# Layer-0 experts and combination: gather rings of eight places instead of four, and another row for the empty places

## The reference

```python
# layer 0, FFN: 32 experts, each token goes to one
logits = xf @ router_w.T + router_b
idx = jnp.argmax(logits, axis=-1)
h = jax.nn.relu(jnp.einsum('nd,ndh->nh', xf, W1[idx]) + b1[idx])      # 256 -> 64
out = jax.nn.relu(jnp.einsum('nh,nhd->nd', h, W2[idx]) + b2[idx])     # 64 -> 256
x = x + out
# layer 1, graph part: three convolutions with the same normalised adjacency A
h1 = layernorm(x) @ W1 + b1 ; n1 = layernorm(relu(A @ h1) + h1) ...
```

## Time and profile before

| | |
|---|---|
| time, median of 3 runs | 2222.27 us (2222.09 to 2224.4) |
| span of the profiled execution | 2275.9 us |
| PE busy | 1915.3 us, 84% of the span |
| DVE busy | 1555.9 us, 68% |
| ACT busy | 1080.4 us, 47% |
| POOL busy | 433.7 us, 19% |

### The profile page before, as it was taken

How to read it: one execution, slowest core, us unless ns; L and a number is a source line. 1 busy time by engine, 2 the same in 40 slices (tenths; PEclk the granted TensorE clock), 3 DMA queues, 4 the chain that set the end, 5 groups by cost and what they waited for, 6 DMA issues and landing times.

```text
span 2275.9 us, 41877 instructions
## 1 busy us (share of the span) xinstructions
PE 1915.3 (84%) x15580; PEld 1273.2 (56%) x15580; DVE 1555.9 (68%) x3262; ACT 1080.4 (47%) x2170; POOL 433.7 (19%) x517
## 2 busy tenths in 40 slices
PE   6999386899999998938994989578867999999787
PEld 3777253678887887826662777456653222222333
DVE  7866654667777667764567557543576999998554
ACT  7555265633443344426674555255554233232654
POOL 0000564100000012216642110055510000000000
PEclk9999688999999999969996999789988999999898
DMA  7999457568888879864567364522232333232000
GB/s 204 309 342 337 114 138 145 201 232 324 310 321 314 308 273 374 332 227 153 191 202 255 105 170 143 181 85 79 73 121 61 119 117 90 82 91 77 1 25 25
DMA packets 238299, 412.55 MB, mean 181 GB/s; under 512 B 20496, under 2 KB 189072, under 8 KB 219857
## 3 DMA queue, kind: packets, MB, share of 16 engines
q1 hardware_dynamic: 214836, 361.52, 47.4%
q0 software_dynamic: 13760, 39.68, 6.5%
q10 hardware_dynamic: 9504, 8.65, 1.2%
HBM read 316.02 MB, written 93.78 MB: 180 GB/s over the span
## 4 chain that ended last, share of the span: by engine, by line
PE 48%; DVE 26%; DMA 9%; ACT 8%; issue 6%; SPq 1%; POOL 1%; ACTq 0%; another core or an unknown queue 0%; DVEq 0%; POOLq 0%
DVE BIG L3024 7%; PE ps L1098 6%; PE ps L1100 6%; PE ps L1099 6%; PE ps L292 5%; PE ps L294 4%; PE ps L293 4%; PE ps L2846 4%; PE ps L2494 4%; DMA BIG<-in_adjT 3%; PE ps L2852 2%; DMA BIG<-in_adj 2%; PE ps L2496 2%; DMA X<-rows_split,idxg 1%; DVE BIG L1644 1%
## 5 line engine op out<-in xcount | busy, mean ns | idle before, releaser
L1098 PE MATMUL ps<-R,BIG 128*128 128x256 f16 (+1 forms) x1764 | 484.1, 274 | 3.0 <-ACT BIG L1539 2.4
L1100 PE MATMUL ps<-R,BIG 128*128 128x256 f16 (+1 forms) x1764 | 481.5, 273 | 0.0
L1099 PE MATMUL ps<-R,BIG 128*128 128x256 f16 x1764 | 481.1, 273 | 0.0
L2846 PE MATMUL ps<-BIG 128*64 128x452 f32 x1056 | 231.2, 559 | 23.9 <-DVE BIG L3024 20.1
L3024 DVE SCALAR_TENSOR_TENSOR BIG<-BIG 128x904 f32<-128x904 f32 x176 | 192.4, 1155 | 1.6
L1098 PEld LDWEIGHTS ps<-R,BIG 128*128 128x128 f16 x1764 | 171.1, 97 | 29.9 <-issue 2.7
L1099 PEld LDWEIGHTS ps<-R,BIG 128*128 128x128 f16 x1764 | 173.1, 98 | 21.2 <-issue 0.3
L1100 PEld LDWEIGHTS ps<-R,BIG 128*128 128x128 f16 x1764 | 171.3, 97 | 23.9
L2908 ACT ACTIVATE BIG<-X,BIG 128x64 f32<-128x64 f32 x264 | 70.2, 337 | 233.8 <-PE ps L2852 233.8
L2557 DVE TENSOR_TENSOR X<-R,X 128x512 f16<-128x512 f32 (+1 forms) x116 | 72.8, 627 | 142.8 <-ACT X L2535 117.0
L2846 PEld LDWEIGHTS ps<-BIG 128*64 128x64 f32 x1056 | 64.5, 137 | 187.4 <-issue 132.0
(11 more groups left out here) (447 smaller groups left out, 4407.3 us busy)
## 6 DMA issues: line engine op xcount, KB each, us to landing
BIG<-adj_split SPq DMA_DIRECT2D x63, 1376.0 KB
BIG<-in_adjT SPq DMA_DIRECT2D x42, 1408.0 KB, 11.8
BIG<-in_adj SPq DMA_DIRECT2D x22, 1408.0 KB
BIG<-in_adjT SPq DMA_DIRECT2D x66, 452.0 KB, 3.3
adj_split<-BIG SPq DMA_DIRECT2D x21, 1376.0 KB
XX<-in_f SPq DMA_DIRECT2D x70, 256.0 KB, 8.8
experts_split<-XX SPq DMA_DIRECT2D x64, 256.0 KB
BIG<-experts_split SPq DMA_DIRECT2D x16, 1024.0 KB
```

The source lines that it names most:

```text
L1098: pe.matmul(out[:, 0:n], pr[:, 0, k, :], h[:, k, 0:n], start=start, stop=False)
L1099: pe.matmul(out[:, 0:D], pr[:, 0, k, :], l[:, k, 0:D], start=False, stop=False)
L1100: return pe.matmul(out[:, 0:n], pr[:, 1, k, :], h[:, k, 0:n], start=False, stop=stop)
L2846: pe.matmul(ps[rs, 2 * (h // 2) + c, 0:CW], self.G[:, u, h * HF:(h + 1) * HF], self.PT[:, u, h, cs], start=start, stop=stop)
```

## The change

- `xg` and `yg1` have eight places each, with a semaphore for each (g0 to g7). Gather j of the experts waits for the transposes of tile j-8, gather t of C0 for the pair (t-8)//2. `xg` takes 1024 more columns of X2, and the work areas behind it move up by as much.
- In the expert stage POOL issues eight gathers, not four, before Degrees and `W[1].pool`.
- An empty place reads the row of its own partition (place p reads row p), in all three routes. That is one more DVE instruction, and one more wait on DVE's own semaphore, ahead of `idxg`.
- Degrees and Many (a small stage of layer 1) use semaphores that other stages also use, in place of six of their own.

```diff
+GATHERED = tuple(f"g{u}" for u in range(8))
-        yg1 = BIG[:, YG:YG + 1024].rearrange("p (u n) -> p u n", u=4)
+        yg1 = BIG[:, YG:YG + 2048].rearrange("p (u n) -> p u n", u=8)
-        xg = work(0, 1024, F16).rearrange("p (u n) -> p u n", u=4)
+        xg = work(0, 2048, F16).rearrange("p (u n) -> p u n", u=8)
...
# C0.pool
-                    if t >= 4:
-                        s.wait(pool, "ta", (t - 4) // 2 + 1)
-                    pool.indirect_dma_start(yg1[:, t % 4, :], None, ys_dram[0:TILES[E0] * P, :],
+                    if t >= 8:
+                        s.wait(pool, "ta", (t - 8) // 2 + 1)
+                    pool.indirect_dma_start(yg1[:, t % 8, :], None, ys_dram[0:TILES[E0] * P, :],
...
# Route.dve; a is -1 at an empty place, pos1 is the partition's number plus 1
                 if A == 1:
-                    v.tensor_scalar(idxg[:, 0:J], a, 0.0, None, ALU.max).then_inc(s["ix"], 1)
+                    link(v.tensor_scalar(c, a, 0.0, pos1[:, 0:1], ALU.is_lt, ALU.mult))
+                    v.tensor_tensor(idxg[:, 0:J], a, c, ALU.add).then_inc(s["ix"], 1)
...
-                v.tensor_scalar(idxg[:, 0:J], b, 0.0, None, ALU.max).then_inc(s["ix"], 1)
+                link(v.tensor_scalar(c, a, 0.0, pos1[:, 0:1], ALU.is_lt, ALU.mult))
+                v.tensor_tensor(idxg[:, 0:J], b, c, ALU.add).then_inc(s["ix"], 1)
...
# Degrees (Many in the same way)
-                self.st = Stage("deg", d=1, r=1, ok=1)
-                self.done = [self.st.end("ok")]
+                self.st = Stage("seq", qp=1, qs=1, pz=1)
+                self.done = [self.st.end("pz")]
...
# Experts0.pool
                 def gather(j):
-                    if j >= 4:
-                        s.wait(pool, "t3", j - 3)
-                    pool.indirect_dma_start(xg[:, j % 4, :], None, xrows[:, :],
+                    s.wait(pool, "t3", j - 7)
+                    pool.indirect_dma_start(xg[:, j % 8, :], None, xrows[:, :],
...
-                for j in range(4):
+                for j in range(8):
                     gather(j)
                 deg.pool(pool)
                 W[1].pool(pool)
-                for j in range(4, self.J):
+                for j in range(8, self.J):
                     gather(j)
```

More of the change, by code:

```diff
@@ L220, in work @@
             return v if dt == F32 else v.bitcast(dt)
-        xg = work(0, 1024, F16).rearrange("p (u n) -> p u n", u=4)
[L223 to L227, removed]
+        xg = work(0, 2048, F16).rearrange("p (u n) -> p u n", u=8)
+        xf = work(2048, 512, F16).rearrange("p (u i n) -> p u i n", u=2, i=4)
+        hact = work(2560, 1024).rearrange("p (u t n) -> p u t n", u=2, t=4)
+        hh = work(3584, 512, F16).rearrange("p (u t n) -> p u t n", u=2, t=4)
+        hl = work(4096, 512, F16).rearrange("p (u t n) -> p u t n", u=2, t=4)
+        yo = work(4608, 1024).rearrange("p (u n) -> p u n", u=4)
         tval = work(0, 2 * KT * JMAX, F16)
@@ L696, in __init__ @@
             def __init__(self, experts, route):
-                n = 16 * (KT // 4)
-                self.st = Stage("seq", g0=n + 16, g1=n + 16, g2=n, g3=n, ta=PR, ag=PR, le=PR, rs=PR, y=PR, t=PR, xh=PR, xl=PR,
+                self.st = Stage("seq", **{g: 16 * len(range(u, KT, 8)) for u, g in enumerate(GATHERED)}, ta=PR, ag=PR, le=PR, rs=PR, y=PR, t=PR, xh=PR, xl=PR,
                                 mm=PR, nn=PR, hh=PR, hl=PR)
@@ L760, in take @@
                     for t in (2 * i, 2 * i + 1):
-                        v.wait_ge(s[f"g{t % 4}"], s.at(f"g{t % 4}") + 16 * (t // 4) + 16)
-                    t, u = 2 * i, 2 * i % 4
+                        s.wait(v, GATHERED[t % 8], 16 * (t // 8) + 16)
+                    t, u = 2 * i, 2 * i % 8
                     if i < PR - 1:
@@ L2165, in __init__ @@
             def __init__(self, prod):
-                self.st = Stage("deg", d=1, r=1, ok=1)
-                self.done = [self.st.end("ok")]
+                self.st = Stage("seq", qp=1, qs=1, pz=1)
+                self.done = [self.st.end("pz")]
             def pool(self, pool):
-                self.st.wait(pool, "d", 1)
-                pool.tensor_tensor(dinv[:, :], degs[:, :], mhalf[:, 0:1].to_broadcast([P, KT]), ALU.pow).then_inc(self.st["r"], 1)
+                self.st.wait(pool, "qp", 1)
+                pool.tensor_tensor(dinv[:, :], degs[:, :], mhalf[:, 0:1].to_broadcast([P, KT]), ALU.pow).then_inc(self.st["qs"], 1)
             def dve(self, v):
@@ L2175, in dve @@
                 v.scalar_tensor_tensor(degs[:, KT - 1:KT], padbig[:, :], 1.0 / 16384, degs[:, KT - 1:KT], ALU.mult, ALU.add)\
-                 .then_inc(s["d"], 1)
-                s.wait(v, "r", 1)
+                 .then_inc(s["qp"], 1)
+                s.wait(v, "qs", 1)
                 v.wait_ge(dv.sem, dv.inc(v.tensor_tensor(dtmp[:, 0, :], degs[:, :], dinv[:, :], ALU.mult)))
@@ L2180, in dve @@
                 v.wait_ge(dv.sem, k)
-                v.scalar_tensor_tensor(dinv[:, :], dtmp[:, 1, :], 1.5, dinv[:, :], ALU.add, ALU.mult).then_inc(s["ok"], 1)
+                v.scalar_tensor_tensor(dinv[:, :], dtmp[:, 1, :], 1.5, dinv[:, :], ALU.add, ALU.mult).then_inc(s["pz"], 1)
         class Many:
             def __init__(self, prod):
-                self.st = Stage("many", mx=1, ar=1, ok=1)
+                self.st = Stage("seq", qp=1, qs=1, pz=1)
                 self.prod = prod
-                self.done = [self.st.end("ok")]
+                self.done = [self.st.end("pz")]
             def pool(self, pool):
-                self.st.wait(pool, "mx", 1)
-                pool.partition_all_reduce(many_f[:, 1:2], many_f[:, 0:1], P, bass.bass_isa.ReduceOp.max).then_inc(self.st["ar"], 1)
+                self.st.wait(pool, "qp", 1)
+                pool.partition_all_reduce(many_f[:, 1:2], many_f[:, 0:1], P, bass.bass_isa.ReduceOp.max).then_inc(self.st["qs"], 1)
             def dve(self, v):
@@ L2199, in dve @@
                     v.wait_ge(z, n)
-                v.tensor_reduce(many_f[:, 0:1], cnt[:, :], AX.X, ALU.max).then_inc(s["mx"], 1)
+                v.tensor_reduce(many_f[:, 0:1], cnt[:, :], AX.X, ALU.max).then_inc(s["qp"], 1)
             def answer(self, v):
                 s = self.st
-                s.wait(v, "ar", 1)
+                s.wait(v, "qs", 1)
                 v.wait_ge(dv.sem, dv.inc(v.tensor_scalar(many_f[:, 2:3], many_f[:, 1:2], float(TOPK_ROWS), None, ALU.is_gt)))
-                v.tensor_copy(many[:, :], many_f[0:1, 2:3]).then_inc(s["ok"], 1)
+                v.tensor_copy(many[:, :], many_f[0:1, 2:3]).then_inc(s["pz"], 1)
         def with_bias(v, s, e, out, both, done):
@@ L2231, in __init__ @@
                 self.J = J = TILES[E0]
-                self.st = Stage("seq", **{f"g{u}": 16 * len(range(u, J, 4)) for u in range(4)}, t3=J, xf=J, hm=J, ha=J, hi=J, lo=J,
+                self.st = Stage("seq", **{g: 16 * len(range(u, J, 8)) for u, g in enumerate(GATHERED)}, t3=J, xf=J, hm=J, ha=J, hi=J, lo=J,
                                 ym=J, yo=J, **{f"w{u}": 16 * len(range(u, J, 4)) for u in range(4)})
@@ L2250, in gather @@
                 def gather(j):
[L2251 to L2256 removed]
+                    s.wait(pool, "t3", j - 7)
+                    pool.indirect_dma_start(xg[:, j % 8, :], None, xrows[:, :],
+                                            bass.IndirectOffsetOnAxis(ap=idxg[:, j:j + 1], axis=0)).then_inc(s[GATHERED[j % 8]], 16)
+                for j in range(8):
                     gather(j)
@@ L2272, in turn @@
                     u = j % 2
-                    s.wait(pe, f"g{j % 4}", 16 * (j // 4) + 16)
+                    s.wait(pe, GATHERED[j % 8], 16 * (j // 8) + 16)
                     s.wait(pe, "xf", j - 1)
```

4 lines of the change are left out of this document (2 added, 2 removed).

## The result

| | median, us | runs | ratio to the kernel before |
|---|---|---|---|
| before | 2222.24 (2222.09 to 2224.4) | 4 | |
| after | 2203.24 (2202.68 to 2208.62) | 4 | 0.9925 [0.9912, 0.9939] |
| after, run again with the last experiments | 2206.46 (2204.89 to 2212.31) | 5 | 0.9939 [0.9925, 0.9952] |

The forecast was 2215.4, its range 2210.0 to 2220.5.

What follows compares the result with a forecast made beforehand. Slow all-row-0 gathers were taken to bound the expert stage's last tiles, gathers and then PE to bound C0. Terms +0.6 + 1.8 - 5.9 - 3.4 = -6.9 us, from 2222.3 to 2215.4 us, range 2210.0 to 2220.5.

Steps and rivals of the forecast that it cites:

- The DVE step: One more DVE instruction ahead of `idxg` in each of three routes: 0.2 us each, +0.6 us; +0.9 at most.
- Eight gathers ahead of Degrees: Start of layer 0's expert stage: power and Degrees later, PE's first result delayed, +1.8 us, bounds 0 and +3.
- Rival 1: DVE gets through between POOL's instructions, so Degrees is free at the expert stage's start: 2213.6 us, chance 0.15.
- The tail: Expert tiles 37 to 51: spread empty rows let the 1.57 us pace replace 1.99, -5.9 us, bounds -5 and -6.3.
- the ring of eight would give nearly the same by itself: Expert tiles 37 to 51: eight gather places alone, without other rows, would end tile 51 about 5.9 us sooner.
- Rival 3: 128 neighbouring rows gather as slowly as one; the ring alone speeds the last expert tiles: 2215.4 us, chance 0.06.
- C0: Gathers from 10 on start earlier, PE's 3.75 us a pair holds from pair 5: -3.4 us, bounds -1.5 and -4.
- Rival 2: C0 gains nothing, the deeper ring only moving the wait: 2218.8 us, chance 0.20.
- Layers 1 and 2: Spread empty rows in the two later routes, four empty tiles of 50: 0 us beyond the added DVE instruction.
- layer 1 starts earlier by what C0 ends earlier: Behind C0: adjacency tiles asked for have landed and the next load waits for PE, so C0's gain stays.
- Rival 4: The gain is taken back in layer 1 by its loads or PE's clock: about 2222 us, chance 0.08.
- rival 5: PE stays cold in the expert stage, 0.57 us more a tile; 2229.7 us with 25 such tiles, chance 0.06.

Runs made afterwards that it cites:

- before, second execution: The kernel before, unchanged, profiled once more for a second trace: 2222.68 us, span 2220.9 us.
- after_again: The changed kernel, no edit, run once more with the last experiments: 2206.46 us, ratio 0.9939 to the kernel before.
- deg_late_dve: The changed kernel with DVE's three last Degrees steps moved behind the whole expert stage in DVE's order: 2208.84 us, ratio 0.9939 to the kernel before.
- rows_ring4: The kernel before with only empty places reading their own partition's row in all three routes, rings of four: 2215.17 us, ratio 0.9969.
- c0_as4: The changed kernel with one wait changed so that C0's gather ring is used as four places: 2211.63 us, ratio 0.9954 to the kernel before.
- own_only_l0_ring8: The changed kernel with empty places of layers 1 and 2 reading row 0 again: 2207.82 us, ratio 0.9938 to the kernel before.
- deg_at4: The changed kernel with Degrees and the weights' low halves behind gather 3 again, rings of eight kept: 2205.72 us, ratio 0.9932 to the kernel before.
- row0_yo8: The changed kernel with empty places reading row 0 again, and eight result places instead of four: 2216.66 us, ratio 0.9980 to the kernel before.
- e0_as4: The changed kernel with the expert stage's gather ring used as four, Degrees after gather 3: 2208.38 us, ratio 0.9937 to the kernel before.
- w1_first: The changed kernel with POOL's order gathers 0 to 3, `W[1].pool`, gathers 4 to 7, Degrees: 2209.89 us, ratio 0.9943 to the kernel before.
- row0_ring8: The changed kernel with empty places reading row 0 again in all three layers, rings of eight kept: 2218.99 us, ratio 0.9990 to the kernel before.
- rows16_ring4: The kernel before with an empty place p reading row p // 8, 16 rows in all, rings of four: 2211.85 us, ratio 0.9950.

## Why the prediction was wrong, point by point

The stage from tile 0 to pair 10 took 140.22 us in before, second execution, and takes 126.82 now: -13.4. The sum's three terms for this stretch were +1.8 - 5.9 - 3.4 = -7.5.

*The DVE step, +0.2 to 0.3 each:* right; 0.28 us for layer 0.

*Eight gathers ahead of Degrees, +1.8:* right in its steps and in size. The power starts at 285.72, 4.7 us later than the earlier trace rows, DVE is held for 3.53 us again, R0 comes 6.57 - 4.79 = 1.78 us later. The bound of up to +3 was needed too: PE's clock reaches 2.4 GHz later, with tiles 4 to 6 spaced 2.14 and 1.30 us. The window 293:298 has a granted clock of 0.96 in before and 0.56 in after. Together 19.24 - 16.49 = +2.75; in after_again, with R0 the same, +3.8, which is outside the bound. Rival 1 is refuted: DVE doesn't get through between POOL's instructions. The rule of the Trainium skill ("SBUF — State Buffer", section "SBUF: two separate sides"), a lock for one instruction, would have let it in at a quarter; after, with Degrees' product, and deg_late_dve, with the low halves, say that DVE is held through all four.

*The tail, -5.9:* this is the step that failed. Its mechanism held, and its size was wrong because of the pace in it. As put there: "the pace of 1.57 us goes on to tile 51: 14 x (1.99 - 1.57)". The 1.99 was right (1.94 in the second execution), and so was its reading as the rate of all-row-0 gathers. But 1.57 was the pace of that one execution, not of the kernel. Two things said so. The span was 53.6 us over the median, and the prediction then took its terms "unscaled". And in the waits of that trace, 306 to 336, DVE stands with nothing to wait for, a row that I passed over and that the second execution doesn't have:

```profile
DVE X L2353 <- issue: 7.0, 13, 1.1
```

With the right pace the same step gives 17 x (1.94 - 1.32) = 10.5 us from tile 34 on, and the tiles 12 to 34 give 30.37 - 29.34 = 1.0 more: -11.6, where -5.9 stood. That is 5.7 of the 5.9 us missing up to pair 10; the start and C0 were off by 1 us each, in opposite directions. With -11.6 in its place the prediction's sum is 2209.7, just below its range, so this term alone doesn't give the measured 2203.24 and 2206.46: the rest came behind pair 10.

The second sentence of this step fell as well, "the ring of eight would give nearly the same by itself". I had PE's pace as the next limit and didn't ask what else uses the full DMA engines, the result writes: with the ring alone the 39 tiles gained 1.0 us, not 5.9, and DVE waited 11.3 us for writes. Rival 3 (the other row doesn't help) is refuted by rows_ring4.

*C0, -3.4:* mechanism right, size a little low: 41.62 - 37.37 = -4.25. The limit behind it is PE's 3.74 us a pair from pair 5, as said; from pair 3 to pair 5, 7.79 us became 6.48, where I had let the gain begin with pair 5. Rival 2 (C0 gains nothing) is refuted by the trace of c0_as4, 42.28 us against 37.37.

*Layers 1 and 2, nothing:* own_only_l0_ring8 agrees within the noise, 1.4 us apart.

*The rest.* By the traces after is 19.9 us shorter than before, second execution: 13.8 at pair 10 (428.00 - 414.21), the rest later. With the instructions of the two lined up, after is 14.5 us ahead at 1000, 16.3 at 1150 and 19.8 at 1240. So the prediction's "layer 1 starts earlier by what C0 ends earlier" held, and 5.3 us came behind it that the sum didn't have. About 3.5 us of them come in the second combination, between 1150 and 1240, where PE's clock rises at another moment. Granted clocks of like stretches, before, second execution, then after (15 us apart in time):

```profile
1190.00:1200.00 10.00, 6.08 (x20) 2.96 (x19) 7.75 (x29) 4.88 (x8) 1.89 (x4) 0.67 0.98 361
1200.00:1210.00 10.00, 7.40 (x34) 3.86 (x33) 9.55 (x31) 5.86 (x10) 2.83 (x6) 0.76 0.54 175
```

```profile
1175.00:1185.00 10.00, 6.08 (x25) 2.85 (x24) 8.99 (x29) 5.48 (x9) 1.89 (x4) 0.83 0.93 346
1185.00:1195.00 10.00, 7.39 (x56) 5.30 (x55) 9.65 (x30) 6.68 (x12) 1.89 (x4) 1.00 0.70 195
```

Relative to before, second execution, after_again, c0_as4, deg_late_dve, deg_at4, own_only_l0_ring8 and row0_yo8 gain 3 to 4 us there as well; rows_ring4, e0_as4, w1_first and row0_ring8, which have edits in common with them, about 1, and rows16_ring4 1.9. It isn't tied to one edit. Both executions of the changed kernel have it, but one or two of each kernel can't say whether the change makes the early rise likelier. That stays open, and with it some 3.5 of the 15 to 19 us. Rival 4 (taken back later) is refuted in any case; rival 5 (PE stays cold) happened for one tile and part of a second, at 1.0 us (2.0 in after_again), not for 12.

## What to carry to other kernels

Padding indices of a gather should not all name one row. Sixteen rows were as good as 128, and the rows took 7.6 us off a stretch where doubling the ring alone took 1.0. The two edits aren't a sum: alone they gave ratios of 0.9969 and 0.9990, together 0.9925 and 0.9939. Here, with the DMA share at 1.0 and few GB/s moved, more buffers moved the wait to the next user of the same engines; what helped was a lower price per transfer. And a pace used as "where it would go without the wait" has to come from an execution whose span stands near the median.

## What the runs showed of the hardware

- A gather of 128 descriptors on one row costs 1.94 us of DMA engines that are full (share 1.01) at 137 GB/s. Spread over 16 or over 128 rows the engines carry 186 to 204 GB/s at shares of 0.64 to 0.76 (330 to 350, rows_ring4, rows16_ring4, after). A packet of such a gather takes 520 ns of its engine, and 170 to 187 ns when spread.
- DVE waits for result writes that share the engines with such gathers, eight of these in flight, up to 2.5 us at a time with four result places and 4.1 us with eight.
- Two kinds of DVE instruction that read two SBUF operands stood until the last of four successive POOL instructions was over (3.53 us for 22 columns, 2.72 us for the two low halves); with those moved away, the same 22 columns take 0.18 us.
- In the second combination, which does the same work in all these kernels, traces are 0.6 to 3.9 us ahead of before, second execution, and in after, 3.5 us ahead, the granted clock stands at 0.83 and 1.00 where before has 0.67 and 0.76.
